# Counts in windows of four nodes, edge rows in pieces of two: the build stage of a graph network on one core

## The reference

```python
dst = jnp.minimum((6250 * uniform ** 2.0).astype(int32), 49999)   # sorted, src reordered with it
h = relu(layernorm(x))
agg_src  = segment_sum(h[src], dst); agg_edge = segment_sum(edge_attr, dst)
x = x + relu(concat([h, agg_src, agg_edge]) @ W.T + b)
h = relu(layernorm(x))
for W_l, b, W_r in two_layers:                  # mean over the edges of a node
    h = relu(segment_sum(h[src], dst) / max(deg, 1) @ W_l + b + h @ W_r)
out = x + h
```

## Time and profile before

| | us |
|---|---|
| median of three runs | 1425.23 (1423.9 to 1428.23) |
| profiled execution | 1426.45, its span 1424.6 |
| mean granted TensorE clock | 0.98 |
| TensorE busy (matmul) | 1352.9, 95% |
| DVE busy | 807.9, 57% |
| ScalarE busy | 492.1, 35% |
| GpSimd busy | 645.4, 45% |

### The profile page before, as it was taken

How to read it: one execution, slowest core, us unless ns; L and a number is a source line. 1 busy time by engine, 2 the same in 40 slices (tenths; PEclk the granted TensorE clock), 3 DMA queues, 4 the chain that set the end, 5 groups by cost and what they waited for, 6 DMA issues and landing times.

```text
span 1424.6 us, 34949 instructions
## 1 busy us (share of the span) xinstructions
PE 1352.9 (95%) x12145; PEld 1227.3 (86%) x12146; DVE 807.9 (57%) x1830; ACT 492.1 (35%) x1398; POOL 645.4 (45%) x762
## 2 busy tenths in 40 slices
PE   3768999999999999999999999999999999999996
PEld 3657999999999999898888888888888888888885
DVE  8678999988988888883445445522222223222122
ACT  2731123455788888882333232311111110000000
POOL 5400001111112122126777776367777654777775
PEclk9688999999999999999999999999999999999998
DMA  6109778888899998895654564656656555666663
GB/s 185 28 4 255 204 221 242 236 250 244 265 273 271 273 280 263 263 278 184 231 184 162 192 222 125 210 180 200 204 188 214 184 184 189 210 216 214 220 219 87
DMA packets 284437, 293.91 MB, mean 206 GB/s; under 512 B 19317, under 2 KB 249920, under 8 KB 284384
## 3 DMA queue, kind: packets, MB, share of 16 engines
q1 hardware_dynamic: 233861, 212.90, 47.6%
q0 software_dynamic: 25728, 68.65, 16.3%
q10 hardware_dynamic: 24795, 11.74, 2.9%
HBM read 245.11 MB, written 48.11 MB: 206 GB/s over the span
## 4 chain that ended last, share of the span: by engine, by line
PE 88%; DVE 4%; ACT 3%; DMA 2%; issue 2%; POOL 2%; ACTq 0%; POOLq 0%; SPq 0%; DVEq 0%
PE edge_banks L1148 42%; PE edge_banks L1084 21%; PE banks L1058 10%; PE edge_banks L1125 4%; PE edge_banks L1080 4%; PE banks L1166 3%; POOL shared L882 2%; PE banks L946 1%; ACT own L1296 1%; DMA shared<-in_edge_attr 1%; PE edge_banks L1155 1%; PE banks L1160 1%; DVE edge_t L1508 1%; ACT shared L1353 1%; DMA shared<-g_rows,list_src 0%
## 5 line engine op out<-in xcount | busy, mean ns | idle before, releaser
L882 POOL DMA_INDIRECT shared<-g_rows,list_src x546 | 532.3, 975 | 232.9 <-issue 166.4
L1148 PE MATMUL edge_banks<-g_even,shared 128*128 128x257 f16 (+1 forms) x3822 | 443.4, 272 | 1.2 <-DVE shared L1776 1.2
L1148 PEld LDWEIGHTS edge_banks<-g_even,shared 128*128 128x128 fp8e3 x3822 | 371.6, 97 | 58.8 <-DVEq L1686 1.3
L1084 PE MATMUL edge_banks<-shared 128*128 128x128 f32 x2744 | 345.3, 276 | 5.2 <-issue 4.3
L1084 PEld LDWEIGHTS edge_banks<-shared 128*128 128x128 f32 x2744 | 325.8, 193 | 8.5 <-issue 8.1
L860 POOL DMA_DIRECT2D counts<-shared x156 | 76.5, 491 | 479.6 <-ACT shared L1353 464.7
L1737 DVE SCALAR_TENSOR_TENSOR shared<-edge_banks,shared,own 128x128 f32<-128x128 f32 x98 | 34.4, 351 | 362.2 <-PE edge_banks L1148 339.5
L1148 PE MATMUL edge_banks<-shared 128*128 128x256 f16 x1911 | 225.8, 272 | 0.2 <-DVE own L1719 0.2
L1653 DVE TENSOR_TENSOR shared<-iota,shared 128x3528 f16<-128x3528 f16 x98 | 195.4, 1994 | 38.9 <-PE banks L1058 38.5
L1353 ACT ACTIVATE shared<-banks 128x392 uint16<-128x392 f32 x312 | 152.1, 487 | 176.0 <-PE banks L1058 165.5
L1148 PEld LDWEIGHTS edge_banks<-shared 128*128 128x128 fp8e3 x1911 | 185.3, 97 | 30.7 <-DVE own L1719 0.5
(11 more groups left out here) (282 smaller groups left out, 978.1 us busy)
## 6 DMA issues: line engine op xcount, KB each, us to landing
shared<-in_edge_attr SPq DMA_DIRECT2D x195, 512.0 KB, 4.7
shared<-counts SPq DMA_DIRECT2D x117, 784.0 KB
counts<-shared POOLq DMA_DIRECT2D x156, 196.0 KB, 4.1
shared<-g_rows,list_src POOLq DMA_INDIRECT x546, 2.6
shared<-hot_rows SPq DMA_DIRECT2D x20, 304.0 KB
g_rows<-g_even SPq DMA_DIRECT2D x1, 3136.0 KB, 15.8
g_rows<-shared ACTq DMA_DIRECT2D x49, 64.0 KB
g_rows<-g_even ACTq DMA_DIRECT2D x49, 64.0 KB
```

The lines of the kernel that those rows point to most:

```text
L882: pool.indirect_dma_start(ring_g[use % RING][:, t, 0:2 * D], None, g_rows[r], bass.IndirectOffsetOnAxis(ap=list_src[:, at:at + 1], axis=0) ...
L1084: mm = pe.matmul(edge_wide[bank][:, :, at], ring[:, bank * GROUP_TILES + j, :], hot_dst[u][:, k, (j - 1) * SPREAD:j * SPREAD].unsqueeze(1) ...
L1148: mm = pe.matmul(acc[s][:, 0:wide], stream8[slot][:, order[h], :], G[r % 2][:, order[h], 0:wide], start=h == 0, stop=h == BLOCKS - 1, skip ...
```

## The change

- `WIN` 8 becomes 4: a step's edges lie in a window of 4 nodes, with 2 x 49 = 98 cells instead of 196. `DUO` 2 becomes 4 and `SLOT` 256 becomes 128, so a bank still holds 16 nodes and ScalarE's evacuation and clearing keep 392 columns. Windows are 1248 instead of 624.
- `STEPS_IT` 18 becomes 20: 10 steps in a half, 1960 in all instead of 1764. `hot_cell` is 20 x 98 columns instead of 18 x 196, `hot_lo` 128 x 20 instead of 128 x 18.
- One wait for `zeroed`, ahead of the ten steps of a half, replaces two.
- Tables of steps grow from 1792 to 2048 entries. Window starts are held in 125 partitions x 10 instead of 112 x 7, for the dense blocks alone; the starts of the ten listed blocks come as one more column (`STARTS` = 12 gathers for 8), which shortens the matmuls at L1004. The key keeps 14 bits for the source and 2 for the node in the window.
- The edge ring takes two neighbouring rows, 1 KB, a piece: a partition holds rows 2p and 2p + 1. The order of destinations in the edge tiles follows, so 13 transposes at L927 become 52 small matmuls.

The diff, cut to its core:

```diff
-WIN = 8
-DUO = 2
+WIN = 4
+DUO = 4
-SLOT = 256
-STEPS_IT = 18
+SLOT = 128
+STEPS_IT = 20
-PARTS = ((0, 5), (5, 9))
+PARTS = ((0, 5), (5, 10))
-PER = 7
+PER = 10
-SRC_BITS = 13
+SRC_BITS = 14
...
+    HOLDERS = -(-DENSE * WINB // PER)
+    MARKS = PER * HOLDERS + P + LISTED
+    STARTS = PER + 2
...
-                    sp.dma_start(ring[:, u * GROUP_TILES:(u + 1) * GROUP_TILES, :], rows.rearrange("(j p) f -> p j f", p=P)).then_inc(batch_landed[u], 16)
+                    sp.dma_start(ring_pairs[:, u * GROUP_TILES // PAIR:(u + 1) * GROUP_TILES // PAIR, :],
+                                 rows.rearrange("(j p k) f -> p j (k f)", p=P, k=PAIR)).then_inc(batch_landed[u], 16)
...
-            for j in range(PER + 1):
+            for j in range(STARTS):
                 pool.indirect_dma_start(rows8[:, j, :], None, keys_table, ...).then_inc(S["rows8_in"], 16)
...
-                    mm = pe.transpose(banks[:, c, j * P:(j + 1) * P], tile_diff[:, 4 * c + j, :], ident[:, :])
+                    to = banks[:, c, j * P:(j + 1) * P]
+                    for k in range(PAIR):
+                        for odd in range(PAIR):
+                            mm = pe.matmul(to[odd * P // PAIR:(odd + 1) * P // PAIR, k::PAIR], tile_diff[:, 4 * c + j, k::PAIR], ident[:, odd::PAIR],
+                                           start=True, stop=True, skip_group_check=True)
...
-                        for j in range(PER):
-                            pe.matmul(to[:, 72 + c:73 + c], pick_j[:, j, lists], first_e[:, j:j + 1], start=j == 0, stop=False, skip_group_check=True)
+                        pe.matmul(to[:, 72 + c:73 + c], pick[:, lists], first_e[0:LISTED, PER + 1:STARTS], start=True, stop=False, skip_group_check=True)
...
-                            for (lo, hi), until in zip(PARTS, regs[HALF:HALF + 2]):
+                            for lo, hi in PARTS:
                                 at = slots(regs[lo:hi])
-                                pe.wait_ge(S["zeroed"], until)
+                                if lo == 0:
+                                    pe.wait_ge(S["zeroed"], regs[HALF])
...
-                        act.activation(duo[j % BANKS], zeros16[:, 0:1].unsqueeze(1).broadcast_to([P, DUO, CELLS]), ACT.Copy).then_inc(S["zeroed"], 2)
+                        act.activation(duo[j % BANKS], zeros16[:, 0:1].unsqueeze(1).broadcast_to([P, DUO, CELLS]), ACT.Copy).then_inc(S["zeroed"], DUO)
```

161 lines of the change are left out of this document (82 added, 79 removed).

## The result

The median of the runs goes from 1426.3 to 1448.3 us, a ratio of 1.0151 with a 95% interval of [1.013, 1.0172]. I had forecast 1427, with a range up to 1444.

The account below looks back on a forecast made before the run. TensorE bounds the kernel, with ScalarE right behind in the last 45% of the build. Terms 0 - 8.3 + 6.4 - 0.5 + 3.9 = +1.5 us took the profiled 1426.45 to 1428.0; predicted median 1427, range 1410 to 1444.

Parts of the forecast that it names:

- Step cost: TensorE's counts in the build: a step of 98 columns takes 0.065 us, bound by its weight load, instead of 0.085.
- Rivals A: TensorE's steps: each costs 0.045 us, the stream and 3 ns; -21 us, 1406 in all; chance 0.20.
- B: TensorE's steps: strided load with its matmul still takes 0.085 us; +21 us, 1448 in all; chance 0.17.
- First stretch: Build up to 408 us, bound by TensorE: 3.9 more quarters (half iterations) +10.3 us, faster quarters -10.2 us, sum 0.
- with the hiccups kept: TensorE's quarters in the build: each saves 0.09 us, 2.65 becoming 2.56, with delays from long register loads unchanged.
- Second stretch: Build from 408 to 644.5 us, bound by ScalarE: 192 duos take 227 us against 235.5 before, -8.3 us.
- 1.5 us for imperfections: Allowance in the build's ScalarE-bound part, over the floor of 225.6 us for 192 duos at 1.175 us.
- merged wait: TensorE's single wait for zeroed banks ahead of ten steps: costed at nothing, as ScalarE still has one complete duo to do.
- rival C: Build's ScalarE-bound part: TensorE restarts late after its single wait, duos stay at 1.22 us; +8.5 us, 1435; chance 0.13.
- Tail: End of the build: 58 padding steps instead of 21 leave 11.6 us after ScalarE's last clear, 5.2 before; +6.4 us.
- Preparation: Work before the first step: more and longer instructions on the chain, +3.9 us, first step at about 117 us.
- off the chain: Preparation work thought hidden: four more POOL gathers landing at 41.4 us, two at L841, and matmuls replacing 13 transposes.

Follow-up runs that it names:

- Fixed columns: Kernel after with all edge tiles at the group's first columns, column unpacking left out; 1974.2 us, ratio 1.0 to the kernel before on another chip.
- shortened clears: Kernel after with ScalarE clearing only 98 of 392 columns of each duo's bank; only the build is read, second stretch 215.7 us.
- early unpacking: Kernel after with an edge group's column arithmetic moved behind the register load of the edge group before, for three of four quarters; 1456.2 us, ratio 1.0215.
- load ahead: Kernel after with the register load for a loop pass's first quarter issued in the edge group before and copied at the head; 1455.7 us, ratio 1.0206.

## Why the prediction was wrong

No single step explains the 16 us: four terms were 2.7 to 4.4 us too low, and the rounds came 2.1 us longer.

**Step cost: right in number, in part by luck.** 0.062 us for 0.065. I had it from the record of the weight load, 0.141 less 0.078 us. The record is now 0.158 us, where I had expected 0.14, and the same subtraction would give 0.080. That the load sets the step is therefore not shown; no run changed the load alone. The clean quarter is 2.46 us; I had 2.49. Rivals A (0.045) and B (0.085) are out, and so is the Trainium skill's 0.081 from "TensorE: Matmul & The Clock Gate", Back-to-back issue gap: at 98 columns and a strided f16 load this trace shows less.

**First stretch: the failed step is "with the hiccups kept".** I took 0.09 us off every quarter. A clean quarter lost more, 0.12 us (2.58 to 2.46), but the means went only from 2.66 to 2.58, and the stretch grew by 2.5 (3.4 over several executions) for -0.5. So the hiccups, mean less clean quarter, weren't kept: they grew from 0.075 to 0.12 us a quarter, 5 us in the stretch. The saving was not to be had where TensorE's sequencer is the bound: at the loop's edge, where all 25 of 25 quarters start their edge group late, and behind some register loads over 1.2 us. The sentence on register loads saw it ("a queue that drains faster has less cover") and then priced it at nothing. Fixed columns put its whole price at 10 us in this stretch. Of the missing 3 us, 2 are a mean saving of 0.07 instead of 0.09 us a quarter, and the rest, the 0.5 for the edge pieces with it, is within the scatter. The earlier trace rows had the loads; a mean by place in the pass would have shown that quarter 0 of before already stood 0.15 us over the rest.

**Second stretch: the mis-sized term is "1.5 us for imperfections".** ScalarE did not reach 1.175 us a duo but 1.205; beyond the floor it was 5.7 us. It waits for TensorE (19 times, 9.0 us) as often as TensorE's matmuls for it (19 times, 7.9 us), and the shortened clears show both within 7% of each other. TensorE's hiccups are not the reason, as far as the runs show: fixed columns and early unpacking moved the first stretch by -10 and +11 us and left the second at 231.2 and 232.3 us. Only the load ahead lengthened it, by 5. So what keeps ScalarE waiting there stays open. The merged wait was rightly costed at nothing: two waits brought 0.6 us. Half of rival C's 8.5 us came, but not by its mechanism.

**Tail: right in kind, 4.0 us short.** From the last wait I gave TensorE six quarters of 2.49 us, 14.9, and ScalarE three duos, 3.3. In after, against the earlier trace rows, TensorE's timeline (edge groups, but for the last, and the last two blocks of steps left out):

```profile
639.37 0.82 PE L1069 MATMUL banks<-shared 128*128 128x98 f16 x10 [0.24 <-ACT banks L1359]
...
642.05 0.81 PE L1069 MATMUL banks<-shared 128*128 128x98 f16 x10
...
645.25 0.84 PE L1069 MATMUL banks<-shared 128*128 128x98 f16 x10
...
647.93 0.77 PE L1069 MATMUL banks<-shared 128*128 128x98 f16 x10
...
650.39 0.78 PE L1069 MATMUL banks<-shared 128*128 128x98 f16 x10
...
654.75 0.83 PE L1069 MATMUL banks<-shared 128*128 128x98 f16 x10 [1.74 <-DVE shared L1672]
...
657.58 0.78 PE L1069 MATMUL banks<-shared 128*128 128x98 f16 x10
...
663.42 1.73 PE L1095 MATMUL edge_banks<-shared 128*128 128x128 f32 x14
```

and ScalarE's last clear:

```profile
649.08 0.50 ACT L1359 ACTIVATE banks<-zeros 128x392 f32<-128x392 f16 x1
```

Six quarters from 647.93 end at 665.2: 17.3 us. One register load of 2.95 us from 651.4 made one of them 4.36 us long (it ended at 654.3, behind VectorE's L1672, which the line names but which ended at 653.9). And ScalarE had one duo left, not three: its last clear ended 1.7 us behind 647.93. The failed step is "from the last wait": TensorE last waited for a zeroed bank at 639.4 us, and its next three quarters took 2.68, 3.20 and 2.68 us without a wait, while ScalarE, with a duo every 1.10 us, caught up. So of the 4.0 us, 2.4 are longer quarters and 1.6 the backlog that wasn't there. Moved padding shows that the tail cost more than every other part, 10.6 of the 22 us.

**Preparation: 6.6 (5.7 over several) for 3.9.** The failed step stands under "off the chain": four more gathers at 1.24 us, landed by 41.4. They took 1.51 us each, the last was issued at 42.1 and landed at 45.4, and VectorE stood in L1540 until 46.4, so L1544 began at 46.5 and not about 43.2. And GpSimd's subtraction behind them, which I did not carry along with the queue, moved from the aggregates onto L1540. L956 then began at 61.3 us, 9.2 later than L946 in the earlier trace rows, where my terms up to there make 5.9; the 3 us between them stayed to the end. The edits that I priced by size came out (L1544 and L1545 1.76 us, L1571 ten times 0.66).

**Edge pieces:** as forecast, between nothing and 2 us.

**Open.** The rounds' code is the same, yet five kernels with steps of 196 columns took 772.9 to 773.9 us for them, and twelve with steps of 98 columns 773.2 to 777.4. The two longest (777.3 and 777.4) were granted half the clock for 3.4 us in the middle of the rounds, after 305 us, which no other had. Up to the last matmul of L1159 (L1148 before) the other ten took 760.4 to 761.2 us and the five 760.1 to 760.3, so most of what is left of the scatter lies in the last 15 us. And the median of after lies 4.2 us over its profiled execution (0 to 3.5 us in nine of its variants), that of the kernels with 196 columns between 0.6 below and 1.6 above. On record, the four runs of after get longer as their mean granted clock falls, from 1444.1 us at 0.980 to 1451.7 at 0.976; the runs of the kernel before show no such order. Why the clock should differ isn't shown; rounds and median together are some 6 us of the 22.

## To carry over

When instructions get shorter, look at what feeds them: here TensorE's sequencer, with address arithmetic and one register load for each 18 matmuls, was a bound right behind the matmuls, and a busy TensorE hid it; leaving out a few register operations showed it. Padding belongs where an engine waits anyway: with 50 steps moved from the end of the loop into the stretch that another engine sets, the tail lost 14.5 us and the stretch grew by 3.9. And when work is added to one queue, follow everything behind it to its new neighbours: an instruction that was free beside one operation stopped another for 3.6 us.

No version beat the kernel before for certain; the edge pieces alone come nearest, at 0.9991 [0.9978, 1.0005].

## Of the hardware, what I had not expected

- A register load of TensorE's sequencer: 12 words 0.85 us at least and 1.06 on the mean, a quarter of them over 1.2; 13 words 2.87 on the mean. With them a quarter took 4.36 us on the mean instead of 2.58.
- GpSimd's tensor_tensor on 128x1651 int32 makes a VectorE scalar_tensor_tensor of 0.21 us last 3.77, a tensor_scalar of 0.16 us last 2.93, and leaves bn_aggr alone.
- An indirect gather of 125 rows costs GpSimd 1.21 us, one of 112 or 128 rows mostly 0.93 to 0.95.
- A strided f16 weight load with a 98-column matmul goes every 0.062 us, though its record lasts 0.158.
- One chip ran the same kernel before in 1975 us instead of 1426. Two variants of the kernel after that were traced there had a mean clock of 0.80 in the rounds, which took them 1302 and 1304 us, while their build ran at 1.00.
